# Two-image MetaFormer block: image 0's attention started ahead of image 1's norm, output sums and first routing placed between attention steps, norms split over ScalarE and VectorE

## The reference

```python
x = x + _L0_conv_ref(_ln_c(x), ...)      # windowed attention, 8 heads, window 8x8, stride 4
t = _to_tokens(x)
t = t + _L0_ffn_ref(_ln_t(t), ...)       # y + sum over 8 experts of combine * (gelu(y w1 + b1) w2 + b2), top 2
x = _from_tokens(t, x)
x = x + _L1_conv_ref(_ln_c(x), ...)      # 1x1 conv to 32, group norm, 9x9 depthwise + 9-tap conv, group norm, 1x1 conv, group norm, + input
t = _to_tokens(x)
t = t + _L1_ffn_ref(_ln_t(t), ...)       # 16 experts, top 2, silu(x w1) * (x w2) times w3
x = _from_tokens(t, x)
```

## Time and profile before

| | us |
|---|---|
| median of 3 runs | 769.71 (768.87 to 771.29) |
| profiled execution, whole time | 768.34 |
| its span on the core | 766.5 |
| start up to the first scores | 0 to 39.1 |
| attention | 39.1 to 171 |
| image 0's output sums and routing up to the first gated step | 171 to 214.6 |
| dense experts | 214.6 to 399 |
| layer three, routing of layer four | 399 to 551.4 |
| layer four's experts and gather | 551.4 to 766.5 |

### The profile page before, as it was taken

How to read it: one execution, slowest core, us unless ns; L and a number is a source line. 1 busy time by engine, 2 the same in 40 slices (tenths; PEclk the granted TensorE clock), 3 DMA queues, 4 the chain that set the end, 5 groups by cost and what they waited for, 6 DMA issues and landing times.

```text
span 766.5 us, 16046 instructions
## 1 busy us (share of the span) xinstructions
PE 561.3 (73%) x5352; PEld 464.2 (61%) x5353; DVE 390.8 (51%) x1109; ACT 321.8 (42%) x761; POOL 389.0 (51%) x445
## 2 busy tenths in 40 slices
PE   0559999976579799999984688335399989999000
PEld 0347777755357577767762466125299989999000
DVE  4856777738472702530046165575655544555521
ACT  0737888871344344552134211222155545555000
POOL 4477999933055676673333000575377007730673
PEclk9999999996599899999995599555599999999555
DMA  8323333324062333331930000012044334442421
GB/s 330 97 63 88 83 94 85 95 77 199 4 210 85 122 130 126 124 112 54 297 101 0 1 1 0 34 53 65 21 125 144 96 97 118 133 115 74 126 81 53
DMA packets 81257, 74.97 MB, mean 98 GB/s; under 512 B 9068, under 2 KB 74820, under 8 KB 80684
## 3 DMA queue, kind: packets, MB, share of 16 engines
q1 hardware_dynamic: 76588, 64.72, 26.5%
q0 software_dynamic: 4608, 9.45, 4.3%
HBM read 50.92 MB, written 23.63 MB: 97 GB/s over the span
## 4 chain that ended last, share of the span: by engine, by line
PE 52%; POOL 16%; DVE 16%; issue 7%; ACT 5%; DMA 3%; SPq 0%; POOLq 0%; DVEq 0%; ACTq 0%
PE bank L743 12%; PE bank L804 8%; PE bank L689 7%; PE bank L705 7%; PE bank L754 6%; POOL gathered_or_att L512 5%; POOL padded_or_w L503 4%; POOL gathered_or_att L571 4%; POOL gathered_or_att L521 3%; PE bank L661 3%; PE bank L259 3%; DVE normed L1029 2%; DVE ln_stats L1007 2%; PE bank L734 1%; PE bank L703 1%
## 5 line engine op out<-in xcount | busy, mean ns | idle before, releaser
L547 POOL TENSOR_TENSOR padded_or_w<-padded_or_w,gathered_or_att 128x384 f32<-128x384 f32 x96 | 95.7, 1006 | 100.4 <-ACT padded_or_w L903 75.5
L559 POOL DMA_INDIRECT sorted_x<-normed,slot x72 | 70.4, 978 | 111.5 <-DVE slot L1196 90.1
L571 POOL DMA_INDIRECT gathered_or_att<-sorted_y,slot x72 | 69.1, 960 | 94.7 <-DMA sorted_y<-padded_or_w 73.3
L903 ACT ACTIVATE padded_or_w<-bank,moe_b 128x384 f32<-128x384 f32 x96 | 55.3, 580 | 119.0 <-PE bank L689 118.9
L705 PEld LDWEIGHTS bank<-moe_or_conv,padded_or_w 128*128 128x128 f32 x576 | 79.8, 196 | 29.1 <-issue 8.3
L689 PE MATMUL bank<-chan_major,moe_or_conv 128*128 128x384 f32 x192 | 81.8, 512 | 2.4 <-ACT padded_or_w L903 2.4
L705 PE MATMUL bank<-moe_or_conv,padded_or_w 128*128 128x128 f32 x576 | 82.4, 281 | 0.0
L1225 DVE TENSOR_TENSOR att_or_moe<-att_or_moe,bank 128x256 f32<-128x256 f32 x104 | 43.7, 420 | 57.1 <-PE bank L754 42.5
L917 ACT ACTIVATE att_or_moe<-bank 128x256 f32<-128x256 f32 x104 | 39.9, 383 | 64.3 <-PE bank L743 63.7
L259 PE MATMUL bank<-consts,normed 128*128 128x128 f32 x144 | 34.2, 373 | 42.1 <-DVE normed L1029 35.4
L743 PE MATMUL bank<-att_or_moe,chan_major 128*128 128x128 f32 x416 | 56.4, 280 | 11.0 <-DVE chan_major L1217 11.0
(11 more groups left out here) (166 smaller groups left out, 1059.0 us busy)
## 6 DMA issues: line engine op xcount, KB each, us to landing
gathered_or_att<-combine SPq DMA_DIRECT2D x24, 768.0 KB, 4.0
padded_or_w<-windows SPq DMA_DIRECT2D x192, 48.0 KB, 2.0
sorted_x<-zeros SPq DMA_DIRECT2D x26, 256.0 KB, 4.4
padded_or_w<-sorted_x SPq DMA_DIRECT2D x26, 256.0 KB
sorted_y<-padded_or_w SPq DMA_DIRECT2D x26, 256.0 KB, 2.4
padded_or_w<-in_moe_w SPq DMA_DIRECT2D x1, 4096.0 KB, 12.1
residual<-in_x_tok SPq DMA_DIRECT2D x2, 1152.0 KB, 6.3
out<-residual SPq DMA_DIRECT2D x12, 192.0 KB, 2.2
```

What stands on the lines that cost most here:

```text
L547: nc.gpsimd.tensor_tensor(HB[n % DRING], HB[n % DRING], GB_[k % 3][:, n % 4, :], ALU.mult).then_inc(S("gated"), 1)
L559: nc.gpsimd.indirect_dma_start(xs_dram[b], bass.IndirectOffsetOnAxis(ap=POS[b][:, k, t:t + 1], axis=0), TN[b][:, t, :], None).then_inc(S(f ...
L571: nc.gpsimd.indirect_dma_start(G[k][:, t, :], None, ys_dram[b], bass.IndirectOffsetOnAxis(ap=POS[b][:, k, t:t + 1], axis=0)).then_inc(S(f" ...
L903: nc.scalar.activation(HB[n % DRING], banks[HBANK[n % 2]][:, 0:DG], ACT.Gelu, bias=B1C[:, e:e + 1]).then_inc(S("gelu"), 1)
```

## The change

- `order` is rewritten. Image 0's norm, `LNA`, keys and edge come first; then the attention steps. Between them stand, by step number: image 1's statistics (0 to 2), norm (2 to 8), transposes, queries and keys (5 to 16), edge (17); output sums and statistics of image 0 (`YA`, `YS`, 12 to 33); norm and routing of image 0 (34 to 46), its choice in six pieces (47 to 52), `RX` (53); five of image 1's six output-sum groups (36 to 53). `AN` of image 0 goes into the dense steps.
- A norm is split into `LN` (the seven small ones), `SQ`, `LV` (reciprocal and a second coefficient, -mean/std) and `LT` by group. A group's `LT` runs on ACT as `activation(Identity, scale, bias)` or on DVE as before, by `on_act`: for `LNA` 0, `XL` 1, `LR` 1 0 and `LR` 1 1 the even groups are on DVE and the odd on ACT; all other norms are wholly on ACT.
- The keys (`KE`) are made by DVE and no longer by ACT; all groups within attention use PSUM bank 0 alone, since bank 1 is the projection's. Logits are one piece (`LG`) behind all transposes, in the same pair of banks.
- SP: image 0's windows and edges first, image 1's windows behind the values of step 8, its right edge behind step 10, its bottom behind step 13; the bottom edge is one DMA, not four. The weights `W12` are loaded in 8 pieces between the gates, not in one.
- Dense steps: the choice of image 1 is in pieces (20 to 26); image 0's layer three starts 4 steps earlier and four of its eight `XU` are within the last dense steps.
- Behind: `XG` of image 1 comes ahead of `GS`, `GQ` and `XUH` of `XU` 0; `slots` of image 0 comes behind `GN XM` 1, with PE's two matmuls (`RP`) behind `GS`.

The core of the diff:

```diff
-        order = [("LN", "LNA", 0), ("SQ", "LNA", 0), *groups("LNA", 0), ("LN", "LNA", 1), ("SQ", "LNA", 1), *groups("LNA", 1), ("EDGE",),
-                 *[("A", n) for n in range(NB * STEPS + 8)],
-                 *groups("YA", 0), *routing(0, 0), *groups("AN", "LR", 0, 0)]
...
+        order += beside("A", 0, shared + 8, [
+            *every(0, 0.5, groups("ST", 1)), (2, ("LN", "LNA", 1)), (2, ("SQ", "LNA", 1)), (3, ("LV", "LNA", 1)), *every(3, 1, groups("LT", "LNA", 1)),
+            *every(5, 2, groups("LNA", 1)), *every(6, 2, groups("KE", 1)), (17, ("EDGE", 1)),
+            *every(12, 4, groups("YA", 0)), *every(13, 4, groups("YS", 0)),
+            (34, ("LN", "LR", 0, 0)), (34, ("SQ", "LR", 0, 0)), (35, ("LV", "LR", 0, 0)), *every(36, 1, groups("LT", "LR", 0, 0)),
+            *every(37, 1.5, groups("RT", 0, 0)), (46, ("LG", 0, 0)), (47, ("RC", 0, 0, 0)), (47, ("RE", 0, 0)), *every(48, 1, choice(0, 0, 1, 6)),
+            (53, ("RX", 0)), *every(36, 4, groups("YA", 1)[:5]), *every(37, 4, groups("YS", 1)[:5])])
+        order += [("YA", 1, NG - 1), ("YS", 1, NG - 1), ("LN", "LR", 0, 1)]
+        order += beside("D", 0, half + DLAG, [
+            (3, ("SQ", "LR", 0, 1)), (3, ("LV", "LR", 0, 1)), *every(5, 2, groups("LT", "LR", 0, 1)), *every(7, 2, groups("RT", 0, 1)),
+            *every(2, 4, groups("AN", "LR", 0, 0)), (19, ("LG", 0, 1)), (20, ("RC", 0, 1, 0)), (21, ("RE", 0, 1)), *every(22, 1, choice(0, 1, 1, 6)),
+            (33, ("RX", 1)), *every(28, 4, groups("AN", "LR", 0, 1))])
...
+            *every(96, 1, [("XU", 0, n) for n in range(4)])])
+        order += [*normed("XL", 1), *[("XU", 0, n) for n in range(4, 8)], ("GN", "XU", 0), *groups("XG", 1), ("GS", "XU", 0), ("GQ", "XU", 0),
...
+                  *choice(1, 0, 1, 6), ("GN", "XM", 1), ("GS", "XM", 1), ("RP", 0), ("GQ", "XM", 1), ("XMH", 1), ("RS", 0),
...
+        def on_act(*ph):
+
+            *ln, g = ph
+            return ln[0] in ("LNA", "LR", "XL") and not (g % 2 == 0 and tuple(ln) in (("LNA", 0), ("XL", 1), ("LR", 1, 0), ("LR", 1, 1)))
...
+            combine_rows(0)
+            sp.wait_ge(S("probs"), NB * STEPS)
+            gates(0)
...
+                for t in range(g * TG, (g + 1) * TG):
+                    ins = nc.scalar.activation(TN[b][:, t, :], XT[b][:, t, :], ACT.Identity, bias=lv[:, 6, t:t + 1], scale=lv[:, 5, t:t + 1])
+                ins.then_inc(S("ln_done_act"), 1)
...
+            def keys(b, g):
+
+                n = group_no[("LNA", b, g)]
+                dve.wait_ge(S("q_ready"), b * NG + g + 1)
+                t_read(ts(KG[b][:, 2 * g:2 * g + 2, 0:NW * Q], t_bank(n)[:, 0:TG * P].rearrange("p (v n) -> p v n", v=2), KW, KB, ALU.mult, ALU.add), n)
```

369 lines of the change are left out of this document (211 added, 158 removed).

## The result

The changed kernel takes **746.63 us** (median; 743.35 to 748.66), the kernel before 770.5 us in the same measurement: a ratio of 0.9684, with a 95% interval of 0.9638 to 0.9729. It is faster by 24 us, where the forecast had 51, and the time lies outside the forecast's range. The profiled execution of the changed kernel has a span of 741.5 us, against 766.5 before, so the two traces show 25.0 us of difference.

The account below looks back on a forecast made before the run. POOL was taken to bound attention and PE the dense steps. Terms -28.3 (with attention's +22 in it), -3.5, -10.5, -7.8 and -0.5 sum to -50.6 from 768.34: 717.7, or 719 as a median; range 702 to 741.

Parts of the forecast that it names:

- step 1: Start of the kernel: image 0's norm halved over two engines, first scores at 28.5 us, a gain of 10.6.
- the wait for values: Early attention: PE's wait of 5.13 us for the first values goes; if they are late, up to 5.1 come back.
- step 3: From attention to first gate: choice free in DVE's idle drain, first gated step at 186.3 instead of 214.6, -28.3 us.
- step 5: Up to image 1's taps: norm tiles halved over two engines, taps at 422.6 us instead of 433.05, -10.5.
- step 6: Slots: the next group norm starts at about 491.4 us and not at 499.22, -7.8; the scatter is late next.
- PE's clock being low through all of attention: Rival: PE falls to its lower clock level in attention, +93 us instead of +22, 790 in all; chance 0.02.
- one sign of being wrong: Attention: the forecast called itself wrong if, among other signs, the granted clock dropped within attention; no size given.
- Step 2: Attention steps: the work moved between them, mostly ACT's excess over its room, costs +22 us, bounds 11 and 38.
- Step 4: Dense steps: the hole of 3.97 us at image 1's choice goes, with another 2.5, against added work; -3.5 us.
- Step 7: The last norm, halved over two engines: -0.5 us, since PE's transposes follow it; experts' loops and gather 0.
- (b): Rival, attention: every piece is a new wait in an in-order list, +40 us instead of +22, 737; chance 0.20.
- (c): Rival, second half: scatter decides or table loads stop gelu, parts 4 to 6 give 8 not 22, 733; chance 0.10.

## Why the prediction was wrong

**Right, within 2 us:** the start (step 1), the wait for values, the tail (step 3: the choice lay free in the drain, as put), image 1's way to the taps (step 5), the slots (step 6: VectorE's two blocks end at 470.2, and what is late next is not the scatter). The run with the routing put back shows that step 3's part carries the gain. No rival that turned on the scatter, or on PE's clock being low through all of attention, came true. But one sign of being wrong did show: the granted clock was 0.51 from 36 to 46 us and 0.57 from 53 to 57 in the changed kernel. The kernel before has transposes at the slow length there too (0.90 us for three at 46.7, 49.7 and 58.0 us, 0.49 at the higher level), so how much of the cost this makes was not separated.

**Step 2, +22, measured +33.** Its method failed. It gave each engine a room per step, its idle time divided by the steps, and priced only what stuck out of the tightest. In the middle it reckoned 7.4 us of VectorE against 13 of room, and added 1; measured: 4.2. The priced pieces show why: PE's and VectorE's cost 0.42 us a group within their room, and they add, because POOL waits for VectorE and VectorE for PE. ScalarE, where the forecast put nearly the whole price, was free in the middle. The bounds of 11 and 38 held the 33; the value taken, 22, was below their middle. Where the 33 us lie is measured: first sixteen steps 12.4, middle 4.2, image 0's routing 15.6, the rest with image 1's sums about 1. Within these, the two steps with a square root take 6.9 and 6.1 us, some 8 us over two steps of 2.4; the forecast had the table loads, but not ScalarE's waits for VectorE between them (3.57 and 1.00 us) with the exponential behind. How the rest of the 15.6 divides between ScalarE (26.33 of 29 us busy there), the one bank and the logits is not settled: spreading the logits over groups or steps took nothing clear away, moving the norms to VectorE made it worse, and sharing them took 1 us off the best run with ScalarE and 7 off the worst.

**Step 4, -3.5, measured +7.6.** The gain was there: with the logits in pieces, first product to fourth sum, where the hole lay, takes 54.0 us, against 60.5 before: 6.5 us, just what the forecast had for the hole. With all losses taken back the whole dense stretch is 7.5 us shorter than before (175.2 against 182.6). The losses were mis-sized, against 3 us in the forecast. Image 1's logits in one piece cost 4.4 us; the forecast had no term for them, having followed the row of 6 and not asked what 36 in a row do. The norms on ScalarE cost 1.9 (1.0 forecast) with the wait in front of PE's transposes. The convolution's half with the table loads costs 6.4 in this stretch, of which 3.7 come back behind it (1.5 forecast); up to 3.4 of the 6.4 is where the clock falls at the end, which differs between runs of the same code. The lower clock is in two of the three.

**Step 7, -0.5, measured +3.5.** The same logits piece again, 1.6 us, at the lower level of the clock (7.86 us for 36 rows). The norm on two engines with its transposes waiting for the slower one accounts for the rest by difference (14.9 against 13.0 before); that was not tried alone.

Logits were wrong in one more way: step 2 has them at 3 x 0.73 us, but 18 tiles are 36 rows, six times 0.73, and 4.18 us in the trace.

**The range.** Rivals (b), the pieces as new waits, and (c), the second half paying back, were each priced alone, 737 and 733. Both came true in good part, together: 719 + 11 + 11 + 4 is 745. They don't exclude each other, and the range should have held their sum.

## What to carry to other kernels

An engine's idle time per step is room for a piece only if the piece doesn't make the bound engine wait: put ahead of what the bound engine is waiting for, and itself waiting for a third engine, a piece costs even where it is shorter than the idle time. So ask of each piece which delivery to the bound engine it stands in front of, before adding up idle times. Send an engine to an instruction whose input comes late, and everything behind it in its list waits too. Gather narrow matmuls into a long piece only where nothing hangs on PE's clock; and where two rivals can both come true, let the range hold both.

## What the runs showed of the hardware

**A long piece of narrow matmuls loses the clock.** PE is listed as busy through all 5.34 us of the 36 rows of 8 columns, with full matmuls on either side, and the granted clock falls within it and is 0.53 from 231 to 238 us. It falls within or close behind this piece in every run that has it, also where the piece itself ran at the higher level throughout (4.08 us), and not at that place in the six profiles with 6 or 18 rows at a time. The Trainium skill, page "TensorE: Matmul & The Clock Gate", section "What's actually happening", ties the clock to how busy PE has been recently. The trace disagrees as far as the listed busy time goes: PE was listed as busy throughout, and the clock fell.

**A table load costs its 1.28 us and no more,** as the forecast had it. ScalarE between two attention steps:

```profile
130.70 0.33 ACT L948 ACTIVATE qy<-bank 128x192 f32<-128x192 f32 x1
131.04 1.28 ACT L890 ACT_TABLE_LOAD   x1
133.33 0.22 ACT L890 ACTIVATE ln_values<-ln_values 128x18 f32<-128x18 f32 x1 [1.00 <-DVE ln_values L1095]
133.56 1.28 ACT L924 ACT_TABLE_LOAD   x1
134.86 0.52 ACT L924 ACTIVATE gathered_or_att<-gathered_or_att 128x384 f32<-128x384 f32 x1
```

The exponential begins 1.30 us behind the start of its load. What costs in addition is that the first load, done early, sits 1.00 us in front of a square root whose input isn't there yet.

**In some of the measurements every kernel took 108 us longer,** the kernel before too, all of it behind 480 us. From the chain of waits of the changed kernel there, at the entry of the first experts' loop:

```profile
570.48 17.45 another core or an unknown queue
587.96 0.38 ACT att_or_moe L988
588.34 8.00 another core or an unknown queue
```

All engines wait there for something that the profile does not name; in the first measurement no such wait stands there. The cause is open. Ratios of whole times from such measurements are drawn towards 1, which is why the comparisons above go by stretches.
